# Moving a quarter of the softmax normalisation, the context copies and two waits in a Flamingo-style kernel

## The chip, the cores and the metric

The kernel runs on one core of a Trainium2 chip. The metric is the device time of one execution in microseconds, lower is better. Durations and starts come from one profiled execution; starts count from the first instruction. TensorE (PE), VectorE (DVE), ScalarE (ACT), GpSimd (POOL) and SyncE (SP) each work through a queue of their own in order, and wait for each other on semaphores.

## The reference, cut to what matters

Four layers, each an attention and a feed-forward part, on x of 32 x 128 x 128, with a context of 32 x 77 x 128, all in float32. The change touches the attention of layer 0 and of layer 3:

```python
# layer 0: 16 heads of 8, queries from the normalised x, keys and values from the context
Q, K, V = heads(LN(x) @ Wq + bq), heads(ctx @ Wk + bk), heads(ctx @ Wv + bv)
attn = softmax(Q @ K.T / sqrt(8))                      # over the 77 context rows
x = x + tanh(g_xattn[0]) * (merge(attn @ V) @ Wo + bo)
# then 8 experts, top 2 of each token, on LN(x)
# layer 3: 8 heads of 128, keys and values from the 77 context rows and the 128 rows of x
kv_in = concat([LN(ctx), LN(x)], axis=1)               # 205 rows
attn = softmax((LN(LN(x)) @ Wq + bq) @ (kv_in @ Wk + bk).T * 128 ** -0.5)
x = x + tanh(g_xattn[3]) * (merge(attn @ (kv_in @ Wv + bv)) @ Wo + bo)
```

## The kernel before, in words

The program is a row of phases with a barrier between them. `head_attention` is layer 0's attention, `sparse_experts` its experts, and `latent_attention` layer 3's attention. Each attention phase walks over the 32 batch elements in a software pipeline written out by hand. In `head_attention`, step b does for each engine the front part for batch b+1 (projections), the middle for batch b (scores, exponentials, sums), the back for batch b-1 (transposed probabilities) and the tail for batch b-2 (output projection, residual). Steps 4 to 11 run in a hardware loop, two to an iteration; the others are unrolled, since they also carry the routing of the first 16 batches to the experts.

The order on each engine is that of the code. For a step of `head_attention` it is as follows.

- PE: transpose of `xn` (L667), scores (L675), heads' outputs (L693, the tail's first part), in routing steps four transposes of `xn_ffn` (L700), projections for V, Q, K (L651, L653, L655), the transposes of the 16 heads' probabilities in four groups (L640, `transposes`), the first before and the second after the matmuls that subtract the maximum (L711), the output projection (L730), then the third and fourth group.
- ACT: `xt` (L470), `heads_out` (L477), `v_padded` (L488), `qt` (L494), transposed probabilities of group 0 (L460), in routing steps `xt_ffn` (L504), exponentials (L508), groups 2 and 3 (L460), in routing steps `xn_ffn` (L521).
- DVE: maximum (L548), masked keys (L556), `xn` for batch b+2 (L560), transposed probabilities of group 1 (L565), residual (L570), routing arithmetic, sum (L611), reciprocal (L614).
- POOL: the copy of batch b+2's context into `context_slot` (L426), the output bias on the residual (L430), from step 24 on three scatters of routed rows to `sorted_x` (L437), then the normalisation of batch b in four groups of four heads (L445), which waits for the reciprocal.

Routing lies in steps 14 to 24: `xn_ffn` in steps 15, 16, 17 and 19, its transposes in 16, 17, 18 and 20 (`TRANSPOSE_STEPS`), the choice of experts in 22 (`PICK`), the ranks in 23 (`COUNT`), and 32 scatters from 24 (`SCATTER`) to 33. The phase ends when its last engine ends.

In those steps PE's second group (bank 5) has to wait for ACT's `xt_ffn`, since `xn_ffn`'s transposes lie in the same bank:

```python
if g == 1 and routes and isinstance(b, int) and b in TRANSPOSE_STEPS:
    pe.wait_ge(s["route_xts"], TRANSPOSE_STEPS.index(b) + 1)
```

In `latent_attention` PE transposes the probabilities of a batch in four parts (L2515: context rows of heads 0 to 3 in bank 6, of heads 4 to 7 in bank 4, x's rows of heads 0 to 3 in bank 5, of heads 4 to 7 in bank 6). ACT copies the first and third (L2274, L2276), DVE the second and fourth (L2387, L2389). Then come, for each half of the heads, a product with the context rows (L2524) and one with x's rows (L2525), both into bank 4 + half. Queries for the next batch (L2535), the output projection (L2543) and the scores (L2475) follow. Steps 2 to 11 are in a hardware loop, the others unrolled.

## Time and profile before

| | |
|---|---|
| device time, median of 3 (lowest, highest) | 1610.8 us (1609.99, 1611.7) |
| the profiled execution | 1607.57 us |
| its span, first to last instruction | 1605.8 us |
| busy share of the span: PE, DVE, POOL, ACT | 86%, 63%, 47%, 46% |
| layer 0's attention | about 23 to 255 us |
| layer 3's attention | about 970 to 1384 us |
| mean granted TensorE clock | 0.932 of full speed |

The span is 1.8 us less than the time of that execution, and its time is 3.2 us below the median. An engine's idle time is put down to what released it ("<-"). A start in the rows further down is that of the first instruction of a group; where more are merged, the duration is from the first start to the last end. Neighbouring instructions of an engine overlap somewhat, so the distance from start to start is the rate at which the engine works.

### The profile page before, as it was taken

How to read it: one execution, taken by the hardware profiler on the slowest of the kernel's cores; microseconds unless marked ns; L12 is line 12 of the kernel's file. 1: busy time of each engine (PE TensorE's matmuls, PEld its weight loads, DVE VectorE, ACT ScalarE, POOL GpSimd, SP SyncE). 2: the span in 40 equal slices, each digit the busy share in tenths (PEclk: the TensorE clock that was granted, in tenths of full speed). 3: DMA queues.
4: the chain of work that ended last, by engine and by line, in shares of the span. 5: the costliest groups of instructions: out<-in, count | busy, mean ns of one | idle time of the engine just before them, and what ended most of it. 6: DMA issues, size and time to landing. Idle time of an engine off the chain costs nothing. (4 is left out here: it accounts for less than half of the span.)

```text
span 1605.8 us, 33990 instructions
## 1 busy us (share of the span) xinstructions
PE 1376.9 (86%) x10919; PEld 1113.0 (69%) x10919; DVE 1004.9 (63%) x2272; ACT 732.2 (46%) x1831; POOL 757.8 (47%) x989
## 2 busy tenths in 40 slices
PE   4998776989765796999989978999999999686996
PEld 2776655989755573777746657778887788486984
DVE  4887872413478386999859964455656655353555
ACT  3677453323266544666645532544554544321121
POOL 2554582244273263555534414445444677116445
PEclk9999898999957796999989998999999999798998
DMA  6400033759310000000000000000000000475943
GB/s 185 196 1 1 10 108 89 213 166 273 93 40 13 1 1 1 1 0 0 1 1 1 0 1 1 1 0 0 1 2 1 16 16 17 128 217 171 301 140 85
DMA packets 96491, 100.09 MB, mean 62 GB/s; under 512 B 12149, under 2 KB 69677, under 8 KB 95726
## 3 DMA queue, kind: packets, MB, share of 16 engines
q1 hardware_dynamic: 62322, 69.60, 14.4%
q0 software_dynamic: 8192, 16.79, 3.5%
q10 hardware_dynamic: 25852, 12.09, 2.7%
q8 instruction: 71, 1.16, 0.3%
q14 instruction: 54, 0.44, 0.1%
HBM read 72.23 MB, written 26.21 MB: 61 GB/s over the span
## 5 line engine op out<-in xcount | busy, mean ns | idle before, releaser
L2235 POOL TENSOR_TENSOR exp_scores_xattn<-exp_scores_xattn,softmax_recip_xattn 128x1640 f32<-128x1640 f32 x32 | 93.5, 2921 | 162.8 <-DVE softmax_recip_xattn L2408 162.8
L1470 PE MATMUL psum<-sorted_transposed_ffn,tile_weights_up_ffn 128*128 128x128 f32 x1280 | 164.1, 283 | 5.2 <-DVE sorted_transposed_ffn L1358 5.1
L1470 PEld LDWEIGHTS psum<-sorted_transposed_ffn,tile_weights_up_ffn 128*128 128x128 f32 x1280 | 153.6, 196 | 12.3 <-DVE sorted_transposed_ffn L1358 12.0
L1244 POOL DMA_INDIRECT gathered_rows_ffn<-sorted_y,slot_ffn x96 | 90.7, 944 | 104.6 <-DMA sorted_y<-expert_rows_ffn 46.1
L799 POOL TENSOR_TENSOR exp_scores<-exp_scores,softmax_recip 128x308 f32<-128x308 f32 x128 | 97.5, 783 | 78.9 <-DVE softmax_sum L893 78.9
L1480 PE MATMUL psum<-expert_weights_down_ffn,hidden_ffn 128*128 x960 | 124.4, 281 | 3.3 <-issue 2.9
L1233 POOL DMA_INDIRECT sorted_x<-xn_ffn,slot_ffn x64 | 61.3, 958 | 132.1 <-DVE slot_ffn L1118 113.2
L445 POOL TENSOR_TENSOR exp_scores<-exp_scores,softmax_recip 128x308 f32<-128x308 f32 x128 | 85.7, 701 | 79.2 <-DVE softmax_recip L614 79.1
L1480 PEld LDWEIGHTS psum<-expert_weights_down_ffn,hidden_ffn 128*128 128x128 f32 x960 | 116.7, 196 | 5.2 <-issue 5.2
L2284 ACT ACTIVATE exp_scores_xattn<-psum,scaled_negated_max_xattn 128x205 f32<-128x205 f32 x256 | 106.6, 451 | 0.0
L2475 PE MATMUL psum<-kv_transposed_xattn,queries_xattn 128*128 128x205 f32 x512 | 98.0, 347 | 3.4 <-DVE queries_xattn L2413 3.4
L640 PE MATMUL psum<-identity,exp_scores 128*77 128x128 f32 x512 | 80.2, 283 | 21.1 <-POOL exp_scores L445 13.5
L2262 ACT COPY kv_transposed_xattn<-psum 128x205 f32<-128x205 f32 x32 | 10.6, 332 | 191.5 <-PE psum L2488 191.5
L1273 ACT ACTIVATE hidden_ffn<-psum 128x512 f32<-128x512 f32 x80 | 47.7, 597 | 110.0 <-PE psum L1470 109.8
L2475 PEld LDWEIGHTS psum<-kv_transposed_xattn,queries_xattn 128*128 128x128 f32 x512 | 91.0, 197 | 4.0 <-DVE queries_xattn L2413 3.9
L933 PE MATMUL psum<-identity,exp_scores 128*77 128x128 f32 x512 | 80.4, 281 | 3.1 <-POOL exp_scores L799 1.1
L640 PEld LDWEIGHTS psum<-identity,exp_scores 128*77 128x77 f32 x512 | 60.6, 151 | 31.2 <-issue 21.5
L1279 ACT ACTIVATE silu_ffn<-psum 128x512 f32<-128x512 f32 x40 | 23.9, 597 | 124.5 <-PE psum L1470 124.5
L2355 DVE TENSOR_REDUCE negated_max_xattn<-psum 128x4 f32<-128x820 f32 x64 | 64.7, 1011 | 25.3 <-PE psum L2475 24.9
L1388 DVE COPY expert_rows_ffn<-psum 128x256 f32<-128x256 f32 x80 | 34.0, 425 | 74.0 <-PE psum L1480 67.6
L1358 DVE COPY sorted_transposed_ffn<-psum 128x256 f32<-128x256 f32 x80 | 33.7, 422 | 72.3 <-PE psum L1448 72.2
L2524 PE MATMUL psum<-probs_t_context_xattn,kv_kept_xattn 77*128 77x512 f32 x128 | 68.0, 612 | 9.2 <-ACT probs_t_latents_xattn L2276 8.4
(391 smaller groups left out, 3639.3 us busy)
## 6 DMA issues: line engine op xcount, KB each, us to landing
tile_weights_up_ffn<-in_L_ffn_packed_dram SPq DMA_DIRECT2D x160, 256.0 KB, 3.4
sorted_rows_ffn<-sorted_x SPq DMA_DIRECT2D x80, 128.0 KB, 4.0
sorted_y<-expert_rows_ffn ACTq DMA_DIRECT2D x80, 128.0 KB
sorted_x<-zeros SPq DMA_DIRECT2D x4, 1280.0 KB, 13.3
x_residual<-in_x_dram SPq DMA_DIRECT2D x4, 512.0 KB, 10.9
expert_weights_down_ffn<-in_L_ffn_packed_dram SPq DMA_DIRECT2D x8, 256.0 KB, 14.6
sorted_x<-xn_ffn,slot_ffn POOLq DMA_INDIRECT x128, 2.3
gathered_rows_ffn<-sorted_y,slot_ffn POOLq DMA_INDIRECT x128, 3.0
```

The lines of the kernel that those rows point to most:

```text
L445: nc.gpsimd.tensor_tensor(e[:, par, heads, :], e[:, par, heads, :], rec.to_broadcast([S, HG, KC]), ALU.mult).then_inc(s["probs_ready"], 1)
L640: last = nc.tensor.transpose(m.psum[0:KC, 4 + g % 2, h * S:(h + 1) * S], e[:, nxt, g * HG + h, :], m.ident[:, :])
L799: nc.gpsimd.tensor_tensor(ev, ev, recip[:, ring % 2, :].unsqueeze(1).to_broadcast([S, HG, KC]), ALU.mult).then_inc(s["probs_ready"], 1)
L933: last = nc.tensor.transpose(m.psum[0:KC, 4 + g % 2, h * S:(h + 1) * S], e[:, (ring - 2) % RING, g * HG + h, :], m.ident[:, :])
L1244: nc.gpsimd.indirect_dma_start(yg[:, n % 4, k, :], None, m.sorted_y[half][:, :], bass.IndirectOffsetOnAxis(slot[:, half, k, b:b + 1], 0)). ...
L1470: mm = nc.tensor.matmul(m.psum[:, 2 * (n % 2) + half, to:to + SUB], w[:, n % DEPTH, u, at:at + 128], xst[:, n % 2, u * SUB:(u + 1) * SUB], ...
L1480: mm = nc.tensor.matmul(m.psum[:, 4 + n % 2, u * D:(u + 1) * D], hid[:, n % 2, c, u * 128:(u + 1) * 128], columns(n, u, c * D), start=(c = ...
L2235: nc.gpsimd.tensor_tensor(ev, ev, recip[:, par, :].unsqueeze(2).to_broadcast([S, H3, KV]), ALU.mult).then_inc(s["probs_ready"], 1)
L2284: ins = nc.scalar.activation(e[:, par, h, :], m.psum[:, h // HB, (h % HB) * KV:(h % HB + 1) * KV], ACT.Exp, scale=SCALE, bias=shift_bias[: ...
L2355: nc.vector.tensor_reduce(negmax[:, par, heads].rearrange("p (n h) -> p n h", h=HB), sv, AX.X, ALU.max, negate=True).then_inc(s["negmax_re ...
L2475: mm = nc.tensor.matmul(m.psum[:, h // HB, (h % HB) * KV:(h % HB + 1) * KV], q[:, par, h, :], kvt[:, par, :], start=True, stop=True)
L2524: nc.tensor.matmul(m.psum[:, 4 + half, :], kept[0:KC, nxt, 0, :], ptc[:, cols], start=True, stop=False)
```

## The change

**Layer 0.** The copy into `context_slot` moves from POOL (ahead of the bias) to ACT (behind group 3) in all steps. On POOL, from step 24 on, the three scatters come behind the normalisation instead of ahead of it. Of batches 24 to 31, POOL normalises groups 0 to 2, and ACT normalises group 3, a step later, in four instructions of one head each, between `qt` and group 0's copy; PE's fourth group and DVE's reciprocal of two batches later wait for them. In steps 22 and 23 (`RELIEF`), ACT makes `xn` (behind `xt`) and copies group 1 (behind the exponentials) in DVE's place. In the four `TRANSPOSE_STEPS`, ACT's `xt_ffn` copy comes ahead of group 0's copy instead of behind it.

**Layer 3.** Before, the first matmul of half 0 waited for both of ACT's copies and the first of DVE's; that of half 1 for all four. Now each product waits for its own operand and for its bank to be free.

```diff
@@ head_attention
+    RELIEF = (PICK, COUNT) if routes else ()
+        def shared(b):
+            return routes and isinstance(b, int) and SCATTER <= b < B
@@ POOL, step
-                    if ahead(b, front):
-                        wait(pool, s["v_in_psum"], b + 1)
-                        nc.gpsimd.tensor_copy(cts[:, par, :], m.ctx_t[:, bass.ds((b + 2) * KC, KC)]).then_inc(s["ct_ready"], 1)
...
+                        for g in range(NG - 1 if shared(b) else NG):
...
@@ ACT, step
+                    if ahead(b, front) and at in RELIEF:
+                        wait(act, s["xt_in_psum"], b + 1)
+                        nc.scalar.activation(xn[:, par, :], m.x[:, b + 2, :], ACT.Identity, scale=m.rstd[:, b + 2:b + 3],
+                                             bias=m.shift[:, b + 2:b + 3]).then_inc(s["xn_ready"], 1)
...
-                    if back:
-                        copy_group(b, 0)
                     if at in TRANSPOSE_STEPS:
...
                         nc.scalar.copy(r.xts[:, g % 2 * GT:(g % 2 + 1) * GT], m.psum[:, 5, :]).then_inc(s["route_xts"], 1)
+                    if back and shared(b - 1):
+                        act.wait_ge(s["recip_ready"], b)
+                        for hd in range((NG - 1) * HG, HEADS):
+                            ins = nc.scalar.activation(e[:, nxt, hd, :], e[:, nxt, hd, :], ACT.Copy, scale=recip[:, nxt, hd:hd + 1])
+                        ins.then_inc(s["probs_by_scalar"], 1)
+                    if back:
+                        copy_group(b, 0)
...
                     if back:
+                        if at in RELIEF:
+                            copy_group(b, 1)
                         copy_group(b, 2)
                         copy_group(b, 3)
+                    if ahead(b, front):
+                        wait(act, s["v_in_psum"], b + 1)
+                        nc.scalar.copy(cts[:, par, :], m.ctx_t[:, bass.ds((b + 2) * KC, KC)]).then_inc(s["ct_ready"], 1)
...
@@ DVE, step
-                    if ahead(b, front):
+                    if ahead(b, front) and at not in RELIEF:
...
-                    if back:
+                    if back and at not in RELIEF:
...
+                        if shared(b - 2):
+                            dve.wait_ge(s["probs_by_scalar"], b - 1 - SCATTER)
@@ PE, transposes
+                    if g == NG - 1 and shared(b - 1):
+                        pe.wait_ge(s["probs_by_scalar"], b - SCATTER)
...
@@ latent_attention, PE
                         for half in range(2):
+                            wait(pe, s["pt_read_act"], b * 2 - 1 + half)
+                            wait(pe, s["pt_read_dve"], b * 2 - 1)
+                            cols = slice(half * 512, (half + 1) * 512)
+                            nc.tensor.matmul(m.psum[:, 4 + half, :], kept[0:KC, nxt, 0, :], ptc[:, cols], start=True, stop=False)
                             wait(pe, s["pt_read_act"], b * 2)
                             wait(pe, s["pt_read_dve"], b * 2 - 1 + half)
-                            cols = slice(half * 512, (half + 1) * 512)
-                            nc.tensor.matmul(m.psum[:, 4 + half, :], kept[0:KC, nxt, 0, :], ptc[:, cols], start=True, stop=False)
                             nc.tensor.matmul(m.psum[:, 4 + half, :], kept[:, nxt, 1, :], ptl[:, cols], start=False, stop=True).then_inc(s["c_in_psum"], 1)
```

What now stands in the engines' queues: first POOL at the end of `head_attention`, before, from step 29 to the last scatter (L430 bias, L437 scatters, L445 normalisation, L426 context copy).

```order
L426 COPY context_slot<-context_transposed 128x77
L430 TENSOR_TENSOR x_residual<-x_residual,L_bo_row 128x128
L437 DMA sorted_x<-xn_ffn,slot_ffn 5120x128 x3
L445 TENSOR_TENSOR exp_scores<-exp_scores,softmax_recip 128x308 x4
L430 TENSOR_TENSOR x_residual<-x_residual,L_bo_row 128x128
L437 DMA sorted_x<-xn_ffn,slot_ffn 5120x128 x3
L445 TENSOR_TENSOR exp_scores<-exp_scores,softmax_recip 128x308 x4
L437 DMA sorted_x<-xn_ffn,slot_ffn 5120x128 x3
L445 TENSOR_TENSOR exp_scores<-exp_scores,softmax_recip 128x308 x4
L437 DMA sorted_x<-xn_ffn,slot_ffn 5120x128 x8
```

The same place of the changed kernel, with its own line numbers (L437 bias, L445 normalisation, L452 scatters).

```order
L437 TENSOR_TENSOR x_residual<-x_residual,L_bo_row 128x128
L445 TENSOR_TENSOR exp_scores<-exp_scores,softmax_recip 128x308 x3
L452 DMA sorted_x<-xn_ffn,slot_ffn 5120x128 x3
L437 TENSOR_TENSOR x_residual<-x_residual,L_bo_row 128x128
L445 TENSOR_TENSOR exp_scores<-exp_scores,softmax_recip 128x308 x3
L452 DMA sorted_x<-xn_ffn,slot_ffn 5120x128 x3
L445 TENSOR_TENSOR exp_scores<-exp_scores,softmax_recip 128x308 x3
L452 DMA sorted_x<-xn_ffn,slot_ffn 5120x128 x11
```

A group and the context copy left POOL's steps, and eleven scatters instead of eight stand behind its last normalisation. Next ACT in one step of the same stretch, before:

```order
L470 COPY xt<-psum 128x128
L477 ACTIVATE heads_out<-psum,L_bias_columns 128x128
L488 COPY v_padded<-psum 77x16x8
L494 ACTIVATE qt<-psum,L_bias_columns 128x128
L460 COPY probs_transposed<-psum 77x512
L508 ACTIVATE exp_scores<-psum 128x1232
L460 COPY probs_transposed<-psum 77x512 x2
```

And ACT in such a step of the changed kernel:

```order
L476 COPY xt<-psum 128x128
L487 ACTIVATE heads_out<-psum,L_bias_columns 128x128
L498 COPY v_padded<-psum 77x16x8
L504 ACTIVATE qt<-psum,L_bias_columns 128x128
L516 ACTIVATE exp_scores<-exp_scores,softmax_recip 128x77 x4
L466 COPY probs_transposed<-psum 77x512
L523 ACTIVATE exp_scores<-psum 128x1232
L466 COPY probs_transposed<-psum 77x512 x2
L532 COPY context_slot<-context_transposed 128x77
```

Four normalising instructions stand between the queries and group 0's copy, and the context copy at the end. The instructions on PE are the same in the same order in both kernels; only its waits differ.

## Rows read from the trace of the kernel before

**Rows 1.** Two stretches: length, busy us of PE, PEld, DVE, ACT, POOL; granted clock.
```profile
192.00:235.00 43.00, 35.85 (x458) 27.28 (x456) 34.56 (x56) 23.78 (x50) 37.26 (x54) 0.98 0.34 102
1000.00:1100.00 100.00, 96.76 (x599) 78.96 (x598) 52.04 (x105) 47.04 (x168) 48.59 (x67) 1.00 0.00 0
```
**Rows 2.** Timeline of POOL, steps 25 and 26: start, duration, instruction, idle before.
```profile
201.13 2.67 POOL L445 TENSOR_TENSOR exp_scores<-exp_scores,softmax_recip 128x308 f32<-128x308 f32 x4
203.75 0.24 POOL L426 COPY context_slot<-context_transposed 128x77 f32<-128x77 f32 x1
...
204.64 1.03 POOL L437 DMA_INDIRECT sorted_x<-xn_ffn,slot_ffn  x1 [0.16 <-issue]
...
208.21 2.68 POOL L445 TENSOR_TENSOR exp_scores<-exp_scores,softmax_recip 128x308 f32<-128x308 f32 x4
```
**Rows 3.** Timeline of POOL, first scatter and first shared step, then the phase's end.
```profile
189.55 1.24 POOL L437 DMA_INDIRECT sorted_x<-xn_ffn,slot_ffn  x1 [0.18 <-issue]
...
194.11 0.69 POOL L445 TENSOR_TENSOR exp_scores<-exp_scores,softmax_recip 128x308 f32<-128x308 f32 x1 [0.79 <-DVE softmax_recip L614]
...
242.45 2.66 POOL L445 TENSOR_TENSOR exp_scores<-exp_scores,softmax_recip 128x308 f32<-128x308 f32 x4
...
254.16 0.95 POOL L437 DMA_INDIRECT sorted_x<-xn_ffn,slot_ffn  x1 [0.30 <-issue]
```
**Rows 4.** Timeline of ACT and, in its last line, PE, in plain steps.
```profile
105.79 0.26 ACT L488 COPY v_padded<-psum 77x128 f32<-77x128 f32 x1 [0.42 <-PE psum L655]
105.95 0.37 ACT L494 ACTIVATE qt<-psum,L_bias_columns 128x128 f32<-128x128 f32 x1
106.21 0.58 ACT L460 COPY probs_transposed<-psum 77x512 f32<-77x512 f32 x1
106.72 1.20 ACT L508 ACTIVATE exp_scores<-psum 128x1232 f32<-128x1232 f32 x1
107.81 0.58 ACT L460 COPY probs_transposed<-psum 77x512 f32<-77x512 f32 x1
108.59 0.58 ACT L460 COPY probs_transposed<-psum 77x512 f32<-77x512 f32 x1 [0.20 <-PE psum L640]
...
111.43 0.37 ACT L494 ACTIVATE qt<-psum,L_bias_columns 128x128 f32<-128x128 f32 x1
...
109.33 0.86 PE L693 MATMUL psum<-probs_transposed,v_padded 77*32 77x128 f32 x24
```
**Rows 5.** Timeline of ACT and, in its last line, PE, in a step with `xt_ffn`.
```profile
121.27 1.65 ACT L521 ACTIVATE xn_ffn<-x_residual,x_second_shift,x_second_rstd 128x128 f32<-128x128 f32 x4
122.82 0.25 ACT L470 COPY xt<-psum 128x128 f32<-128x128 f32 x1
...
125.22 0.60 ACT L504 COPY xt_ffn<-psum 128x512 f32<-128x512 f32 x1
...
125.91 0.53 PE L640 MATMUL psum<-identity,exp_scores 128*77 128x128 f32 x3 [0.69 <-issue]
```
**Rows 6.** Timeline of PE and DVE in step 22, then DVE in step 23.
```profile
167.83 0.39 PE L730 MATMUL psum<-L_wo,heads_out 128*128 128x128 f32 x2
...
168.06 0.68 DVE L565 COPY probs_transposed<-psum 77x512 f32<-77x512 f32 x1
...
180.26 0.69 DVE L565 COPY probs_transposed<-psum 77x512 f32<-77x512 f32 x1 [1.46 <-PE psum L640]
```
**Rows 7.** Waits of PE in layer 3's attention: total us, times, longest.
```profile
PE psum L2524 <- ACT probs_t_latents_xattn L2276: 8.4, 30, 0.4
```
**Rows 8.** Timeline in layer 3: a loop step, an unrolled step, DVE's copy and PE.
```profile
1064.83 0.69 DVE L2387 COPY probs_t_context_xattn<-psum 77x512 f32<-77x512 f32 x1
...
1065.99 0.69 PE L2524 MATMUL psum<-probs_t_context_xattn,kv_kept_xattn 77*128 77x512 f32 x1 [0.41 <-ACT probs_t_latents_xattn L2276]
...
1256.24 0.68 DVE L2387 COPY probs_t_context_xattn<-psum 77x512 f32<-77x512 f32 x1
...
1257.28 0.67 PE L2524 MATMUL psum<-probs_t_context_xattn,kv_kept_xattn 77*128 77x512 f32 x1 [0.21 <-ACT probs_t_latents_xattn L2276]
```

25 lines of the change are left out of this document (14 added, 11 removed).

## The prediction, made before the changed kernel ran

> **What bounds the kernel now.** I read the busy time of stretches first, then the timeline of each engine in one step of the kind that the change touches, then the list of waits. In layer 3's attention PE is busy 96.8 of 100 us at full clock, and no other engine more than 52 [rows 1]: what PE idles there is what can be had. Nearly all waits of its first context product are for ACT's copy of x's rows, 8.4 us in 30 of 32 batches [rows 7]. They come in two sizes, 0.41 us in the ten loop steps and 0.21 in the twenty unrolled ones that waited for ACT [rows 8]. In layer 0's attention there are several regimes. In plain steps ACT starts on `qt` every 5.48 us (105.95 to 111.43) and has gaps [rows 4]; PE sets the pace there. In the `TRANSPOSE_STEPS` PE stands still for 0.69 us before the second group of transposes [rows 5]. From step 24 POOL is the bound: 37.3 us busy in 43 without the gaps between its scatters [rows 1], and one normalisation follows the next after 7.08 us with no wait for the reciprocal [rows 2]. POOL also ends the phase, at 254.16 + 0.95 = 255.11 [rows 3].
>
> **Layer 3: the split waits.** Nothing is added or removed but waits. The first product needs ACT's first copy, DVE's first copy (it reads the bank that the product overwrites) and the end of the transposes. In the unrolled step DVE's copy ends at 1256.24 + 0.68 = 1256.92, while PE fell idle at 1257.28 - 0.21 = 1257.07, so the product can follow the transposes at once: the 0.21 goes. In the loop step DVE's copy ends at 1065.52 and PE fell idle at 1065.58. These are close, and a wait in the loop may take a little longer to be seen; I take back 0.33 of the 0.41, with 0.2 and 0.41 as bounds. ACT's second copy is then wanted only behind two matmuls of the first product, which take over 0.8 us, long after it has landed. Sum: 10 x 0.33 + 20 x 0.21 = 7.5 us. PE's gain is everybody's only where PE is next in line; in the few steps with routing arithmetic DVE or POOL ends last, so I take off 1.0 as an estimate: **-6.5 us**. Bounds: 4.2 (the unrolled steps alone) and 8.4 (all of rows 7). The added waits are for things long done, and are hidden behind the running matmul. If DVE is late, this cover is gone and the wait is only renamed.
>
> **Layer 0: the shared steps.** POOL's step was 4 groups at 0.655 = 2.62 ((203.75 - 201.13)/4 each), context copy and bias 0.89 with their gaps (203.75 to 204.64), and three scatters 3.57 (to 208.21) [rows 2]. Now it is three groups 1.96, a gap of 0.17, scatters 3.57, bias 0.45: 6.15 us instead of 7.08. But what is late next? The chain through ACT: from `qt` to group 0's copy 0.26; from there to group 3's copy without its idle 2.08 (0.51 + 1.09 + 0.48); from that to PE's heads' outputs 0.74 (108.59 to 109.33); and on to the next `qt` 2.10 (109.33 to 111.43). That is 5.18 us [rows 4], to which four normalising ACTIVATEs are added between `qt` and group 0's copy, 4s. No row has this form. Bounds for s: 0.16, the distance from a copy without operands per partition to the next instruction (105.79 to 105.95) [rows 4], and 0.39, that of four ACTIVATEs with two such operands and 128 columns ((122.82 - 121.27)/4) [rows 5]. The nearest row is `qt`, one such operand and 128 columns, 0.26 [rows 4]; I take that. The chain is 6.22, just above POOL's 6.15, so a step takes 6.22.
>
> The Trainium skill (ScalarE: Activation LUTs, "What ACT_TABLE_LOAD costs") gives an ACTIVATE 186 ns + 0.833 per column + 93 per pointer operand, less 93 back to back; for 77 columns and one pointer that is 250 ns, which puts the chain at 6.18 and the sum 0.2 us lower. The trace agrees for two pointers and 128 columns: it shows 0.39 between starts, the page gives 386 ns.
>
> The price of the new order: batch 24's three scatters no longer fill POOL's idle time ahead of 194.11 (from 189.55 [rows 3]) but come behind, so eleven scatters instead of eight are left after the last normalisation. Before, the last part took 255.11 - 242.45 = 12.66. One group less (-0.66), three scatters more at 0.96 + 0.30 = 1.26 (+3.78) and no other change: 15.78. From batch 25's normalisation at 201.13: five steps of 6.22, a last one of 5.70 (no bias, no queries), then 15.78: 201.13 + 31.1 + 5.7 + 15.8 = 253.7, against 255.1: **-1.4 us**. With s = 0.16 POOL's 6.15 binds: -1.8. With s = 0.39 the step is 6.74: +1.2.
>
> A scatter can cost more in its new place. The first one took 1.24 us [rows 3], the one of step 25 1.03 [rows 2]; I count 0 and keep 0.2 a step, some +1.4 in all, as the other end. The Trainium skill (SBUF — State Buffer, "Who interferes with whom") says that VectorE in a two-port mode and GpSimd lock each other out for a whole instruction; by it, `xn` on DVE, now beside the first scatter of a step, would make the higher price the rule. The sum would be -0.0 instead of -1.4.
>
> **Layer 0: smaller edits.** `xt_ffn` ahead of group 0's copy starts one copy (about 0.5 us) earlier. PE's wait of 0.69 falls to 0.2, in four steps: **-2.0 us** (bounds 0 and 4 x 0.69 = 2.8). Group 0's copy comes later by as much, but PE wants it only behind the second group, and the exponentials start where they did. The context copy leaves POOL, where in plain steps it lay in idle time, for ACT. In plain steps it stands behind group 3's copy; the next thing on ACT's chain waits for PE, so it is hidden; it also delays `xt` by 0.16, which PE wants only behind the heads' outputs. In steps 14 to 19, ACT goes from there to table loads and `xn_ffn`, for which PE waits: 6 x 0.16 = **+1.0** (bounds 0 and 1.5). The first copy delays the first `xt` by 0.16: **+0.2**. The relief of DVE: in step 22 its copy ends at 168.74 while the output projection that the residual needs ends at 168.22 [rows 6], so the chain of routing comes some 0.4 earlier: **-0.4**. In step 23 DVE had waited 1.46 us before that copy [rows 6]: PE is late there, nothing is won. ACT has room for both instructions.
>
> **Sum.** Layer 3 -6.5, layer 0 -1.4 - 2.0 + 1.0 + 0.2 - 0.4 = -2.6: -9.1 us. The span of 1605.8 becomes 1596.7, the profiled execution's 1607.57 becomes 1598.5. That execution lies 3.2 below the median of 1610.8; the median becomes **1601.7**.
>
> **The rivals.**
> 1. ACT binds the shared steps, or the scatters grow dearer, or the context copy delays more than counted: with s = 0.39 layer 0 gives 0.0 in all, and 1604.3 comes out. For it: the chain and POOL are within 0.1 us of each other, so any slip shows. Against: one pointer operand and 77 columns should cost less than that row.
> 2. In layer 3 the wait is renamed: DVE's first copy, or what a wait in the loop costs, takes the place of ACT's. Then the loop gives 0 and the unrolled half, 2.1; with layer 0's 2.6 that is 1606.1. Against: in the unrolled step DVE's copy ended 0.15 before PE fell idle [rows 8].
> 3. More than forecast: all of the 8.4, and layer 0 with POOL's pace, 2.8 for the copies and little for the context: -13, 1597.8.
> 4. Slower, by one mechanism: the four normalising ACTIVATEs on ACT's chain. The stretch breaks even where six steps take 41.3 - 3.1 = 38.2 us together, a step of 6.45 us (s = 0.32). To eat also the other gains of 7.7 us and 3.2 us more, the step must be 8.3 us, s = 0.78. At s = 0.8 the time is 1614.5. No ACTIVATE of this width is that slow in the rows.
> 5. The change doesn't do what it says: neither stretch is set by what I name, and the gains fall into slack elsewhere: 1609.
>
> **How the numbers follow.** Chances: forecast 0.48, rival 1 0.20, rival 2 0.13, rival 3 0.10, rival 4 0.05, rival 5 0.04. The range from 1597.0 to 1606.5 takes in rivals 1 to 3 and the bounds of layer 3's term with either end of layer 0's, and leaves out rivals 4 and 5 and the edges of 2 and 3, under 2 in 10. A difference of 0.2% (3.2 us) is about what a measurement can tell from none, so faster means under 1607.6: forecast, rivals 1 and 3 whole but for 0.01, and 0.10 of rival 2: 0.87. The same: the rest of these and rival 5: 0.08. Slower: 0.05.
>
> **What would show it.** In layer 3, PE's waits before its first context product fall from 8.4 us to under 2, a loop step loses 0.3 us, an unrolled one 0.2, and PE waits nowhere anew. In layer 0, normalisations on POOL follow each other after 6.2 us, POOL waits a little for the reciprocal in most of these steps, the four ACTIVATEs are 0.26 apart, and POOL ends about 2.6 us earlier than 255.1. The 0.69 us before the second group falls to 0.2. Wrong would be: a new PE wait for DVE of 0.2 or more in layer 3; ACT's normalisations over 0.39 apart; plain steps of layer 0 longer than 5.5 us, which would put the context copy on their path.

## The result, and the profile of the changed kernel

| | before | after |
|---|---|---|
| median of 6 runs each (lowest, highest) | 1610.35 us (1608.38, 1611.7) | 1598.91 us (1597.44, 1603.12) |
| profiled execution, and its span | 1607.57, 1605.8 us | 1598.82, 1596.8 us |
| mean granted TensorE clock of that execution | 0.932 | 0.931 |

The ratio of the mean times is 0.9937, with a 95% interval from 0.9927 to 0.9948: faster by 10.1 us (8.4 to 11.8); the medians lie 11.4 apart. The forecast was 1601.7 with a range from 1597.0 to 1606.5, so the median lies inside it, 2.8 us under the forecast. The profiled execution of before was a quick one: its 1607.57 us lie below the lowest of the six runs. Measured again, the changed kernel gave a median of 1597.66 us over five runs, without a sixth of 1708.03 us that ran at a lower granted clock (0.81).

Layer 3 first. These are PE's waits for ACT in the changed kernel's layer 3, where [rows 7] had 8.4 us in 30 (total us, times, longest):

```profile
PE psum L2550 <- ACT probs_t_latents_xattn L2302: 1.3, 7, 0.2
```

No wait for DVE has taken its place. The timeline of a loop step around the first context product (start, duration) shows why. It answers the first two lines of [rows 8]:

```profile
1061.26 1.93 PE L2541 MATMUL psum<-identity,exp_scores_xattn 128*77 128x128 f32 x16
...
1062.43 0.69 DVE L2413 COPY probs_t_context_xattn<-psum 77x512 f32<-77x512 f32 x1
1062.77 0.59 ACT L2302 COPY probs_t_latents_xattn<-psum 128x512 f32<-128x512 f32 x1 [0.29 <-PE psum L2541]
1063.22 0.69 DVE L2415 COPY probs_t_latents_xattn<-psum 128x512 f32<-128x512 f32 x1
...
1063.27 1.10 PE L2550 MATMUL psum<-probs_t_context_xattn,kv_kept_xattn 77*128 77x512 f32 x2
...
1064.20 1.02 PE L2553 MATMUL psum<-probs_t_latents_xattn,kv_kept_xattn 128*128 128x512 f32 x2
```

The transposes end at 1063.19 and DVE's copy at 1063.12; the product starts at 1063.27, while ACT's second copy is still running (to 1063.36). That second copy is wanted only at 1064.20. So ACT is off the path, and DVE is just not on it: 0.07 us were left. In the unrolled step PE goes from transposes to product without a gap:

```profile
1249.21 1.98 PE L2541 MATMUL psum<-identity,exp_scores_xattn 128*77 128x128 f32 x16
1251.18 1.10 PE L2550 MATMUL psum<-probs_t_context_xattn,kv_kept_xattn 77*128 77x512 f32 x2
```

From the first start of a batch's context products to that of the next batch it was 12.40 us in the loop before and is 12.10 now (12.15 and 12.05 in turn); in an unrolled step it was 12.24 and is 12.02. From PE's first scores of the phase to the start of its last output projection it was 408.0 us and is 400.6.

Layer 0. First the busy time of the two stretches of [rows 1] (length; busy us of PE, PEld, DVE, ACT, POOL; granted clock):

```profile
192.00:235.00 43.00, 39.69 (x479) 30.03 (x479) 35.16 (x60) 32.99 (x89) 35.49 (x46) 0.99 0.33 103
1000.00:1100.00 100.00, 98.79 (x616) 80.78 (x615) 56.92 (x110) 48.27 (x174) 48.49 (x66) 1.00 0.00 0
```

PE goes from 35.85 to 39.69 and from 96.76 to 98.79, ACT in layer 0 from 23.78 to 32.99. A shared step on POOL, in the place of [rows 2], and the last scatter of the phase, in that of [rows 3]:

```profile
213.20 2.00 POOL L445 TENSOR_TENSOR exp_scores<-exp_scores,softmax_recip 128x308 f32<-128x308 f32 x3
215.36 1.01 POOL L452 DMA_INDIRECT sorted_x<-xn_ffn,slot_ffn  x1 [0.16 <-issue]
216.68 0.96 POOL L452 DMA_INDIRECT sorted_x<-xn_ffn,slot_ffn  x1 [0.30 <-issue]
217.94 0.96 POOL L452 DMA_INDIRECT sorted_x<-xn_ffn,slot_ffn  x1 [0.30 <-issue]
218.92 0.47 POOL L437 TENSOR_TENSOR x_residual<-x_residual,L_bo_row 128x128 f32<-128x128 f32 x1
219.34 2.01 POOL L445 TENSOR_TENSOR exp_scores<-exp_scores,softmax_recip 128x308 f32<-128x308 f32 x3
...
252.20 0.95 POOL L452 DMA_INDIRECT sorted_x<-xn_ffn,slot_ffn  x1 [0.30 <-issue]
```

Normalisations follow each other after 219.34 - 213.20 = 6.14 us instead of 7.08, with no wait for the reciprocal, and POOL ends at 253.15 instead of 255.11. The same step on ACT, with the new row L516:

```profile
213.97 0.37 ACT L504 ACTIVATE qt<-psum,L_bias_columns 128x128 f32<-128x128 f32 x1
214.23 1.10 ACT L516 ACTIVATE exp_scores<-exp_scores,softmax_recip 128x77 f32<-128x77 f32 x4
215.23 0.57 ACT L466 COPY probs_transposed<-psum 77x512 f32<-77x512 f32 x1
...
217.73 0.27 ACT L532 COPY context_slot<-context_transposed 128x77 f32<-128x77 f32 x1
...
220.09 0.37 ACT L504 ACTIVATE qt<-psum,L_bias_columns 128x128 f32<-128x128 f32 x1
```

The four ACTIVATEs take (215.23 - 214.23)/4 = 0.25 us each, and the next `qt` comes 6.12 us after this one. POOL and ACT go at the same pace, within 0.02 us.

What the rows do not show by themselves is how much each part gave: the start of layer 3 moved by only 0.5 us (974.2 to 973.7) although POOL's scatters end 2.0 us earlier. The experiments take the parts apart.

### The profile page after: what moved, and what is told of

It reads as the page before. It is cut to its first block and busy times, and to the rows that moved or that the text cites. A ratio compares the mean times of both kernels' runs of the same rounds, so it can differ in the third digit from the quotient of the medians.

```text
span 1596.8 us, 34083 instructions
## 1 busy us (share of the span) xinstructions
PE 1382.9 (87%) x10919; PEld 1118.7 (70%) x10919; DVE 1009.6 (63%) x2268; ACT 742.6 (47%) x1899; POOL 746.9 (47%) x949
## 3 DMA queue, kind: packets, MB, share of 16 engines
q8 instruction: 71, 1.16, 0.3%
## 5 line engine op out<-in xcount | busy, mean ns | idle before, releaser
L825 POOL TENSOR_TENSOR exp_scores<-exp_scores,softmax_recip 128x308 f32<-128x308 f32 x128 | 97.6, 785 | 79.6 <-DVE softmax_sum L919 79.6
L445 POOL TENSOR_TENSOR exp_scores<-exp_scores,softmax_recip 128x308 f32<-128x308 f32 x120 | 80.5, 702 | 91.0 <-DVE softmax_recip L637 91.0
L855 ACT COPY probs_transposed<-psum 77x512 f32<-77x512 f32 x96 | 56.0, 587 | 42.2 <-PE psum L959 41.6
```

Source lines behind the costliest of these rows:

```text
L445: nc.gpsimd.tensor_tensor(e[:, par, heads, :], e[:, par, heads, :], rec.to_broadcast([S, HG, KC]), ALU.mult).then_inc(s["probs_ready"], 1)
L825: nc.gpsimd.tensor_tensor(ev, ev, recip[:, ring % 2, :].unsqueeze(1).to_broadcast([S, HG, KC]), ALU.mult).then_inc(s["probs_ready"], 1)
```

## The experiments

Layer 0 is read below by the starts of DVE's reciprocal of each batch (L614 before, L637 after). The table has the distances between them in us: "4 to 13" is from that of batch 4 to that of batch 13.

| kernel | 4 to 13 | 13 to 15 | 15 to 20 | 21 to 22 | 23 to 24 | 25 to 31 | 31 to the end of the last scatter |
|---|---|---|---|---|---|---|---|
| before | 51.21 | 12.66 | 36.39 | 8.20 | 8.05 | 40.42 | 14.22 |
| after | 51.87 | 12.82 | 35.24 | 7.80 | 8.58 | 35.98 | 16.71 |
| the changed kernel again | 51.89 | 12.81 | 35.25 | 7.81 | 7.87 | 36.03 | 16.8 |
| filler copy on POOL | 51.01 | 12.81 | 35.24 | 7.81 | 8.79 | 35.93 | 16.7 |
| context copy on POOL | 51.22 | 12.65 | 34.45 | 7.82 | 7.87 | 35.96 | 16.7 |
| first trio early | 51.91 | 12.81 | 35.24 | 7.81 | 7.87 | 35.84 | 12.94 |
| two operands per partition | 51.86 | 12.81 | 35.24 | 7.81 | 8.69 | 38.16 | 16.15 |
| no relief | 52.05 | 12.82 | 35.23 | 8.20 | 8.77 | 35.99 | 16.7 |
| only `xt_ffn` moved | 51.03 | 12.66 | 34.45 | 8.20 | 8.79 | 40.09 | 14.2 |
| scatters ahead | 52.01 | 12.82 | 35.23 | 7.80 | 7.87 | 35.85 | 12.9 |
| four scatters early | 51.01 | 12.65 | 34.46 | 7.80 | 8.78 | 35.83 | 11.67 |

All the kernels with 51.0 to 51.2 in the first column have a copy of 77 columns on POOL ahead of the bias add, all with 51.9 to 52.1 have none. The kernel of the first experiment below, whose layer 0 is that of before, has 51.00; the 51.21 of before holds one step of 6.07 us (batch 5 to 6) that took 5.92 there. That step takes one or the other in kernels of either kind, so 0.15 us in this column tell nothing.

**Layer 3's waits alone.** The kernel before, with:

```
 for half in range(2):
+    wait(pe, s["pt_read_act"], b * 2 - 1 + half)
+    wait(pe, s["pt_read_dve"], b * 2 - 1)
+    cols = slice(half * 512, (half + 1) * 512)
+    nc.tensor.matmul(m.psum[:, 4 + half, :], kept[0:KC, nxt, 0, :], ptc[:, cols], start=True, stop=False)
     wait(pe, s["pt_read_act"], b * 2)
     wait(pe, s["pt_read_dve"], b * 2 - 1 + half)
-    cols = slice(half * 512, (half + 1) * 512)
-    nc.tensor.matmul(m.psum[:, 4 + half, :], kept[0:KC, nxt, 0, :], ptc[:, cols], start=True, stop=False)
     nc.tensor.matmul(m.psum[:, 4 + half, :], kept[:, nxt, 1, :], ptl[:, cols], start=False, stop=True)
```

> The kernel before with one part of the change: layer 3's split waits, nothing in layer 0. Theory: this part is worth what the phase showed in the trace of the changed kernel, 7 to 7.5 us between PE's first scores and its last output projection of layer 3 (it was forecast at 6.5), so the time is 1603 us, and PE's waits ahead of the first context product fall from 8.4 us to under 2. Rival: part of the 11.4 us by which the medians differ comes from a TensorE clock that falls and rises elsewhere; then this kernel gains either much less than 6 us or nearly all of it.

Measured: 1602.09 us against 1609.67 for the kernel before beside it, ratio 0.9954 (0.9940 to 0.9967). Layer 3 takes 400.4 us from first scores to last output projection. PE's wait is the same as in the changed kernel:

```profile
PE psum L2524 <- ACT probs_t_latents_xattn L2276: 1.3, 7, 0.2
```

The theory holds: this part is worth 7.4 us by the ratio (5.3 to 9.7) and 7.6 by the medians.

Its layer 0 is the same code as in the kernel before, so it also shows how two executions of that code differ: from batch 0 to 1 it takes 5.94 us here and 5.05 there, from 2 to 3 5.48 and 6.09, from 23 to 24 8.78 and 8.05, and the last scatter ends at 255.90 here and at 255.11 there.

**Layer 0's edits alone.** The changed kernel with the lines above put back.

> The changed kernel with layer 3's two waits put back as they were, so that only the edits of layer 0 are left. Theory: POOL's last scatter of layer 0 ends at 253.2 us as in the changed kernel, 2.0 us earlier than before, and the time is 1608.3 us, 2 to 2.5 us under the kernel before; with the layer-3 kernel of this call the two gains add up to the whole. Rival: layer 0's gain is lost in the routing and the experts behind it, and the time is 1610, or it is larger than 2.5 because a later stretch runs at a higher granted clock.

Measured: 1606.58 us against 1609.67, ratio 0.9980 (0.9971 to 0.9989), that is 3.1 us (1.8 to 4.7) less. Its reciprocals lie within 0.1 us of the changed kernel's throughout, its last scatter ends at 253.18. Layer 3 takes 407.8 us, and the old wait is there again (8.2 us in 29). The two parts add up: 7.6 + 3.1 = 10.7, and the whole gave 10.1 (8.4 to 11.8). The trace of before and that of the changed kernel had shown only 2.0 us on POOL's end; against the 255.90 of the experiment above it is 2.7.

**The context copy, and what it had been good for.** Two kernels, both on the changed one. The first makes POOL copy the context once more to an unused tile in the steps below 24; a semaphore of its own orders the copies. The second puts the copy that counts back on POOL for these steps, and leaves ACT's from step 24 on:

```
 def step(b, par, front, middle, back, tail):          # POOL, first kernel
+    if ahead(b, front) and not (isinstance(b, int) and b >= SCATTER):
+        wait(pool, s["v_in_psum"], b + 1)
+        wait(pool, s["spare_done"], b + 1)
+        nc.gpsimd.tensor_copy(spare[:, par, :], m.ctx_t[:, bass.ds((b + 2) * KC, KC)]).then_inc(s["spare_done"], 1)
```
```
 def step(b, par, front, middle, back, tail):          # POOL, second kernel
+    if ahead(b, front) and not (isinstance(b, int) and b >= SCATTER):
+        wait(pool, s["v_in_psum"], b + 1)
+        nc.gpsimd.tensor_copy(cts[:, par, :], m.ctx_t[:, bass.ds((b + 2) * KC, KC)]).then_inc(s["ct_ready"], 1)
...
-    if ahead(b, front):                               # ACT
+    if ahead(b, front) and isinstance(b, int) and b >= SCATTER:
         wait(act, s["v_in_psum"], b + 1)
         nc.scalar.copy(cts[:, par, :], m.ctx_t[:, bass.ds((b + 2) * KC, KC)]).then_inc(s["ct_ready"], 1)
```

> The changed kernel with one POOL copy more in each step below 24: the transposed context is copied once more, to a tile that nobody reads, where the kernel before had its context copy. ACT keeps the copy that counts. Theory: in the changed kernel the bias add on POOL follows the normalisations at once and meets DVE's xn (0.62 us there instead of 0.40), which makes DVE's copy of group 1 and then PE late; with the filler the bias add starts 0.45 us after the normalisations as it did before, xn falls back to about 0.40, and the plain steps 0 to 13 take 0.08 to 0.09 us less each, 1.2 us in all. In the steps 14 to 19 nothing comes back, since there it is ACT that is late: time 1597.7. Rival: the plain steps grew because ACT has one instruction more in the loop, with its address taken from a register; then they stay as they are, the reciprocal of batch 13 starts at 110.6 and not at 109.5, and the time is 1598.9.

Measured: 1600.18 us, ratio 0.9939 (0.9924 to 0.9953). From batch 4 to 13 it takes 51.01 us instead of 51.87. The reciprocal of batch 13 comes at 110.14, not at 109.5 as the theory had it. Batch 1 came 0.4 us later in this execution (42.17 against 41.81), and from there to batch 13 it is 0.85 us less, not the 1.1 that this would need. First a plain step of the changed kernel on DVE, POOL and PE, then the same with the filler; the last line of each is PE's fourth group of transposes:

```profile
73.30 0.62 DVE L581 TENSOR_SCALAR xn<-x_residual,x_rstd,x_shift 128x128 f32 x1
73.85 0.67 DVE L586 COPY probs_transposed<-psum 77x512 f32<-77x512 f32 x1
...
73.39 0.46 POOL L437 TENSOR_TENSOR x_residual<-x_residual,L_bo_row 128x128 f32 x1
...
74.65 0.66 PE L666 MATMUL psum<-identity,exp_scores 128*77 128x128 f32 x4 [0.38 <-DVE probs_transposed L586]
```
```profile
73.49 0.40 DVE L586 TENSOR_SCALAR xn<-x_residual,x_rstd,x_shift 128x128 f32 x1
73.84 0.69 DVE L591 COPY probs_transposed<-psum 77x512 f32<-77x512 f32 x1
...
73.56 0.25 POOL L438 COPY spare_slot<-context_transposed 128x77 f32 x1
73.77 0.45 POOL L442 TENSOR_TENSOR x_residual<-x_residual,L_bo_row 128x128 f32 x1
...
74.66 0.66 PE L671 MATMUL psum<-identity,exp_scores 128*77 128x128 f32 x4 [0.20 <-DVE probs_transposed L591]
```

In the changed kernel the bias add starts 0.09 us after `xn` and ends at 73.85; `xn` ends at 73.92. DVE's copy of group 1 comes later by 0.2, and PE idles 0.38 instead of 0.20 before the fourth group. With the filler it is the copy that starts 0.07 after `xn`. It ends at 73.81 and `xn` at 73.89. So `xn` is late here too, but beside an instruction of 0.25 us and not beside one of 0.46, and takes 0.40. Useless work on POOL thus gives the plain steps 0.86 us back, all that they had lost (51.01 against the 51.00 of the kernel with layer 3's edit alone). That ACT has one instruction more in the loop costs nothing there, since it is still there in this kernel. The first theory holds in kind, with 0.9 us instead of 1.2; the rival falls. In the steps 14 to 19 nothing comes back (12.81 and 35.24), as expected. The time does not show the 0.9 us: the median is 1.3 above the changed kernel's, and its runs spread from 1596.69 to 1601.27.

> The changed kernel with the context copy back on POOL in the steps below 24 and on ACT from step 24 on, where POOL is the bound. Theory: the plain steps give back 1.2 us and the steps 14 to 19 another 1.0 (0.16 each), the shared steps stay at 6.13 us; the last scatter of layer 0 ends at 251.0 instead of 253.2 and the time is 1596.7. Rival: the copy on ACT cost the steps 14 to 19 nothing, and only the 1.2 come back: 1597.7. Second rival: what is won in layer 0 is lost again where the granted clock falls in the stretches between the layers: 1598.9.

Measured: 1599.05 us, ratio 0.9938 (0.9924 to 0.9952). The plain steps give back 0.65 us, or 0.80 without the step from batch 5 to 6, which is one of 6.07 us here; the steps 14 to 19 0.17 + 0.79 = 0.96, or 0.16 for each, and the shared steps stay at 36.0. So the copy on ACT does cost what was forecast there. The last scatter ends at 250.16, 3.0 us earlier than in the changed kernel: 1.6 of these come from the copies, 0.7 from the distance of batch 23 to 24 (7.87 against 8.58, which the next experiment shows to be chance), and the rest from batches 0 to 4. The median shows none of it. In this execution layer 1's attention starts at 441.5, and in the changed kernel's at 442.8, so 1.3 are left. But from the experts' first transposes to there the same code took 183.8 us in one execution and 185.1 in another (next), so that loss can't be put down to the edit. Whether 1.6 us reach the end stays open with this kernel alone.

**The changed kernel again,** unedited.

> The changed kernel as it is, measured again beside the three kernels of this call. Every reading of this study says the same: 1599 us. If it comes out over 1.5 us from that, differences of that size between calls mean nothing, and only kernels of one call are to be compared.

Measured: 1597.66 us, ratio 0.9924 (0.9911 to 0.9937), 1.2 us under 1598.91. So medians that were not taken side by side may be compared down to about 1.5 us and no further. The table shows what differs between these two executions of the same code: in no step from batch 1 to 23 more than 0.05 us, and then 0.7 us from batch 23 to 24. PE's rows in that step, of the changed kernel and then of the repeat (the matmuls that subtract the maximum and a group of transposes, the same instructions in both):

```profile
188.84 1.00 PE L737 MATMUL psum<-negated_max,identity_bf 128*128 128x308 bf16 x4 [1.56 <-DVE negated_max L569]
189.64 1.06 PE L666 MATMUL psum<-identity,exp_scores 128*77 128x128 f32 x4
```
```profile
189.94 0.71 PE L737 MATMUL psum<-negated_max,identity_bf 128*128 128x308 bf16 x4 [1.56 <-DVE negated_max L569]
190.49 0.60 PE L666 MATMUL psum<-identity,exp_scores 128*77 128x128 f32 x4
```

The same transposes take 1.06 us in the first and 0.60 in the second. Between 188 and 192 us the granted clock is 0.64 of full speed in the first and 1.00 in the second. PE had idled in both just before (1.56 us). Of the eleven kernels of the table four show 7.87, six 8.58 to 8.79 and one 8.05, with no pattern in their edits, and the unedited kernel shows both. The same holds for the stretch from the experts' first transposes to layer 1's attention: 183.8 us and 185.1.

**Where the scatters stand.** Two kernels on the changed one. One moves every trio one step earlier, so that the first is issued ahead of batch 24's normalisation. The other puts each trio back ahead of the normalisation of its own step, as before the change:

```
+if routes and isinstance(b, int) and b == SCATTER:     # first kernel, ahead of "if middle:"
+    ...
+    scatter(0, PER_STEP)
 if middle:
     ...
-    for pair in range((b - SCATTER) * PER_STEP, ...):
+    scatter((b - SCATTER + 1) * PER_STEP, min(2 * HBATCH, (b - SCATTER + 2) * PER_STEP))
```

> The changed kernel with every trio of scatters one step earlier: the first three stand ahead of batch 24's normalisation, in POOL's idle time, as they did before the change, and eight instead of eleven are left behind the last normalisation. Theory: the shared steps stay at 6.13 us, the last scatter ends 3 x (0.96 + 0.30) = 3.8 us earlier, at 249.4 instead of 253.2, and PE's wait for the first sorted rows shrinks with it; time 1595.2. Rival: the steps ahead of batch 24 are not POOL's, and the scatters come so late that they push batch 24's normalisation back by up to 3.6 us; then nothing is won, 1599. Second rival: POOL ends earlier as said, but the experts behind it run at a lower granted clock, as with the context copy on POOL (3.0 us earlier there, of which 1.3 were left at 441 us), and half is left: 1597.

Measured: 1594.55 us (1592.11 to 1595.85) beside 1597.66 for the changed kernel, ratio to before 0.9902 (0.9889 to 0.9915). From the last reciprocal to the end of the last scatter it takes 12.94 us instead of 16.71, that is 3.8 less, and the shared steps do not get longer. The medians differ by 3.1 and the means by 3.9, so nearly all of it, as far as these runs can tell, reaches the end. POOL in this kernel, around batch 24:

```profile
188.05 1.16 POOL L441 DMA_INDIRECT sorted_x<-xn_ffn,slot_ffn  x1 [0.18 <-issue]
189.52 0.97 POOL L441 DMA_INDIRECT sorted_x<-xn_ffn,slot_ffn  x1 [0.30 <-issue]
190.79 0.96 POOL L441 DMA_INDIRECT sorted_x<-xn_ffn,slot_ffn  x1 [0.30 <-issue]
192.62 2.01 POOL L453 TENSOR_TENSOR exp_scores<-exp_scores,softmax_recip 128x308 f32<-128x308 f32 x3 [0.86 <-DVE softmax_recip L640]
```

The trio fits into the wait for the reciprocal with 0.86 us to spare. Both rivals fall.

> The changed kernel with each trio of scatters ahead of the normalisation of its step, as before the change; the last group is still ACT's. Theory: POOL does the same work in each shared step in either order, and the steps stay at 6.13 us; the first trio lies in POOL's idle time and eight scatters are left at the end instead of eleven, so POOL ends 3.8 us earlier and the time is 1595, as with the trios moved by one step. Then to put the scatters behind cost 3.8 us and bought nothing. Rival: with the scatters ahead, the probabilities of a batch come 3.6 us later in the step, PE waits for them, and the step becomes longer than POOL's 6.13, at 0.5 us a step by all of the 3.8: time 1599.

Measured: 1594.51 us, ratio 0.9914 (0.9898 to 0.9930). POOL in two shared steps:

```profile
206.55 2.01 POOL L452 TENSOR_TENSOR exp_scores<-exp_scores,softmax_recip 128x308 f32<-128x308 f32 x3
208.53 0.45 POOL L437 TENSOR_TENSOR x_residual<-x_residual,L_bo_row 128x128 f32<-128x128 f32 x1
209.14 1.01 POOL L444 DMA_INDIRECT sorted_x<-xn_ffn,slot_ffn  x1 [0.17 <-issue]
210.45 0.96 POOL L444 DMA_INDIRECT sorted_x<-xn_ffn,slot_ffn  x1 [0.30 <-issue]
211.71 0.95 POOL L444 DMA_INDIRECT sorted_x<-xn_ffn,slot_ffn  x1 [0.30 <-issue]
212.68 2.02 POOL L452 TENSOR_TENSOR exp_scores<-exp_scores,softmax_recip 128x308 f32<-128x308 f32 x3
```

The step is 212.68 - 206.55 = 6.13 us, as with the scatters behind, and 12.9 us are left after the last reciprocal. So the new place of the scatters bought nothing in this kernel and cost 3.8 us; the gain of the shared steps comes from the fourth group on ACT (0.66 us of POOL's step by [rows 2]) and the context copy off POOL (0.24). No kernel takes these two apart in the shared steps.

**How close ACT's chain is.** The changed kernel with a second operand per partition, a bias of zero, on ACT's normalisation (the values are the same):

```
-ins = nc.scalar.activation(e[:, nxt, hd, :], e[:, nxt, hd, :], ACT.Copy, scale=recip[:, nxt, hd:hd + 1])
+ins = nc.scalar.activation(e[:, nxt, hd, :], e[:, nxt, hd, :], ACT.Identity, scale=recip[:, nxt, hd:hd + 1], bias=m.zeros[:, 0, 0:1])
```

> The changed kernel with a dearer form of ACT's normalising instruction: Identity with a bias of zero that is read per partition, two operands per partition instead of one, same values. Measured now: starts 0.25 us apart; with two operands 0.34 to 0.39. Theory: ACT's chain of 5.18 + 4s (5.18 from the rows of before) is then 6.54 to 6.74 us, longer than POOL's 6.13, so the steps of batches 25 to 31 take that, POOL waits 0.4 to 0.6 us for the reciprocal in each, and its last scatter ends 2.5 to 4 us later than 253.2: time 1602. This would show that the chain lies just under POOL in the changed kernel and how steep the loss is where it takes over. Rival: the chain has more slack than its rows say, since PE and DVE overlap parts of it; then the steps stay at 6.13 and the time at 1599.

Measured: 1599.60 us beside 1597.66, ratio to before 0.9939 (0.9926 to 0.9952). ACT in one step, and POOL's wait in it:

```profile
214.86 0.37 ACT L504 ACTIVATE qt<-psum,L_bias_columns 128x128 f32<-128x128 f32 x1
215.12 1.47 ACT L516 ACTIVATE exp_scores<-exp_scores,zeros,softmax_recip 128x77 f32<-128x77 f32 x4
216.48 0.57 ACT L466 COPY probs_transposed<-psum 77x512 f32<-77x512 f32 x1
...
221.34 0.37 ACT L504 ACTIVATE qt<-psum,L_bias_columns 128x128 f32<-128x128 f32 x1
```
```profile
219.98 2.01 POOL L445 TENSOR_TENSOR exp_scores<-exp_scores,softmax_recip 128x308 f32<-128x308 f32 x3 [0.29 <-DVE softmax_recip L637]
```

The price is (216.48 - 215.12)/4 = 0.34, the step 221.34 - 214.86 = 6.48, and 6.48 - 4 x 0.34 = 5.12: the chain without the ACTIVATEs. At 0.25 that makes 6.12, just below POOL's 6.13. So the theory holds in kind: the chain starts to bind right where the changed kernel stands, and from there each 0.01 us on all four ACTIVATEs costs 0.04 us a step. That it binds is shown; the slope is worked out from these two kernels and not measured at a third price. The step is 0.06 shorter than 5.18 + 4s gave, the last scatter ends at 254.68, 1.5 later than 253.15, where at least 2.5 had been expected, and the time moved by 1.9 instead of 3. The range of the runs (1598.37 to 1602.03) overlaps that of the changed kernel, so the time alone would not show it.

**The two small edits.** In one kernel the relief is off (`RELIEF = ()`), on the changed kernel. In the other, `xt_ffn`'s copy ahead of group 0's is the only edit, on the kernel before:

```
-if back:
-    copy_group(b, 0)
 if at in TRANSPOSE_STEPS:
     ...
     nc.scalar.copy(r.xts[:, g % 2 * GT:(g % 2 + 1) * GT], m.psum[:, 5, :]).then_inc(s["route_xts"], 1)
+if back:
+    copy_group(b, 0)
```

> The changed kernel without the relief of VectorE: in steps 22 and 23, xn and group 1's copy are DVE's again, as before the change. Theory: in step 22 they lie ahead of the residual and the routing arithmetic and cost 0.4 us there, nothing in step 23: the reciprocal of batch 22 comes 7.8 + 0.4 us after that of batch 21, and the time is 1599.3, which no median can tell from 1598.9. Rival: DVE waits anyway, and the distance stays at 7.8.

Measured: 1599.20 us, ratio 0.9940 (0.9927 to 0.9952). From batch 21 to 22 it takes 8.20 us instead of 7.80. The theory holds: the relief is worth 0.4.

> The kernel before with one edit: the copy to xt_ffn stands ahead of group 0's copy on ACT. Theory: PE's wait of 0.69 us before the second group of transposes falls to 0.2 in four steps, and from the reciprocal of batch 15 to that of batch 20 it takes 34.4 us instead of 36.4 (in the changed kernel 35.2, of which 0.8 were for the context copy): time 1607.7. Rival: the edit wins nothing by itself, and the shorter steps 16 to 19 of the changed kernel have another cause; then 36.4 stays.

Measured: 1606.43 us against 1609.90, ratio 0.9984 (0.9975 to 0.9993), or 2.6 us (1.1 to 4.0). From batch 15 to 20 it takes 34.45 instead of 36.39. PE's second group, where [rows 5] had 0.69, and ACT's copy ahead of it:

```profile
125.76 0.63 PE L640 MATMUL psum<-identity,exp_scores 128*77 128x128 f32 x4 [0.21 <-issue]
...
125.08 0.58 ACT L502 COPY xt_ffn<-psum 128x512 f32<-128x512 f32 x1
125.55 0.59 ACT L460 COPY probs_transposed<-psum 77x512 f32<-77x512 f32 x1
```

The theory holds: -1.94 us in four steps.

**Better than both.** The context copy on POOL below step 24 and the scatters one step earlier, then the same with four scatters in the gap instead of three:

```
+scatter(0, PER_STEP + 1)                    # at SCATTER, ahead of the normalisation
 ...
+scatter((b - SCATTER + 1) * PER_STEP + 1, 2 * HBATCH if b == B + 1 else (b - SCATTER + 2) * PER_STEP + 1)
```

> The changed kernel with the context copy on POOL below step 24 and each trio of scatters one step earlier. Theory: the gains on POOL add, 3.0 and 3.8 us, and the last scatter ends at 246.4 instead of 253.2; by the time that is 1592 if all of it stays. Rival: the experts and the stretches behind them give back what they gave back with the context copy alone, over half, through the granted clock; then the phase of the scatters ends at 246.4 and the time is 1596.

Measured: 1594.87 us, ratio 0.9899 (0.9886 to 0.9912), as with the scatters alone (1594.55). Neither the theory's 1592 nor the rival's 1596 came out. The last scatter ends at 248.2, not at 246.4. The parts are there (51.02, 34.46 and 12.96 us in the columns of the table), but this execution had the longer step from 23 to 24 (8.79), and batch 1 came 1.5 us later than with the scatters alone. The expectation had taken 3.0 us for the context copy, of which 1.6 were the copy's.

> The kernel with the context copy on POOL below step 24 and the first scatters in POOL's idle time, with four of them there instead of three, so that seven are left behind the last normalisation. Theory: the fourth just fits (4 x 1.27 = 5.1 us in a gap of 5.4) and pushes batch 24's normalisation back by 0.5 at most; from the last reciprocal to the end of the last scatter it takes 11.7 us instead of 12.9, and the time is 1593.8. Rival: the granted clock behind it takes it back: 1594.9 as measured with three.

Measured: 1591.52 us (1591.16 to 1592.76, four runs), ratio 0.9887 (0.9872 to 0.9901). That is the best of all, 2.3 us under the forecast of 1593.8, and its interval does not touch the changed kernel's. From the last reciprocal it takes 11.67 us. POOL:

```profile
191.66 0.96 POOL L444 DMA_INDIRECT sorted_x<-xn_ffn,slot_ffn  x1 [0.30 <-issue]
193.12 2.01 POOL L456 TENSOR_TENSOR exp_scores<-exp_scores,softmax_recip 128x308 f32<-128x308 f32 x3 [0.50 <-DVE softmax_recip L643]
```

Even the fourth scatter fits with 0.50 us to spare, so batch 24 is not late at all. Against the same kernel with three scatters the edit is worth 1.3 us by the trace (12.96 against 11.67); the medians lie 3.3 apart, but their intervals overlap, and why they differ by more than 1.3 is not shown.

## Why the prediction was right, point by point

**Layer 3: right in mechanism, sized 0.9 too small.** Forecast -6.5, measured -7.4 (400.6 against 408.0). The prices per step held: 0.30 in a loop step (forecast 0.33), 0.22 in an unrolled one (0.21); 10 x 0.30 + 20 x 0.22 = 7.4. The step that failed is the 1.0 taken off for the steps with routing arithmetic. The longest of these took 13.86 us before and 13.62 after: they gained like the others. PE's wait fell to 1.3 us (forecast under 2).

**The shared steps: right.** From batch 25's normalisation to the end of the last scatter the forecast was 31.1 + 5.7 + 15.8 = 52.6; it is 253.15 - 200.91 = 52.2, against 53.98 before. So the term is -1.7 instead of -1.4. The price s is 0.25 (forecast 0.26), the chain without it 5.12 (5.18). One term of that chain, the last 0.48 of 2.08, stands in no row: from one copy to the next [rows 4] have 108.59 - 107.81 = 0.78, of which 0.20 are idle, so 0.58. With 0.58 the chain would have been 5.28, further from the 5.12 that the dearer ACTIVATE showed. The binding engine changed with these hundredths: I had ACT just above POOL and POOL waiting a little in most steps; in the changed kernel POOL does not wait, and only the kernel with the dearer ACTIVATE shows the wait. The price of the order was right: 15.79 us after the last normalisation (forecast 15.78), and the two kernels that move the scatters showed that this 3.8 us was given away. The prediction had counted it but not asked what it bought.

The Trainium skill (ScalarE: Activation LUTs, "What ACT_TABLE_LOAD costs") gives a rule from which 250 ns follow for this form and 343 ns for two pointer operands, back to back; these are estimates, and the traces agree, with 0.25 and 0.34.

**`xt_ffn`: right.** Forecast -2.0, -1.94 as the only edit. PE's gap fell to 0.21 (forecast 0.2).

**The context copy: right in the steps 14 to 19, wrong in the plain ones.** Forecast +1.0 there, and 0.96 measured. In the plain steps I counted nothing, since I looked at what the copy does on ACT. The step that failed is the one not made: what its going from POOL does. It made the bias add start with `xn`, and six of the twelve `xn` between 50 and 115 us took 0.61 to 0.63 us instead of at most 0.47. That is 0.7 us from batch 4 to 13 against before, 0.9 against the filler and against the kernel with layer 3's edit alone, and 0.9 is the better figure, since the 51.21 of before holds the longer step from 5 to 6. The forecast had this collision for the scatters of the shared steps, and not for the bias add. The +0.2 for the first `xt` can't be seen: the first reciprocal starts anywhere between 35.66 and 36.59.

The Trainium skill (SBUF — State Buffer, "Who interferes with whom") says that VectorE in a two-port mode and GpSimd hold the shared pair of ports for a whole instruction, and that the other blocks. The trace agrees for `xn` beside the bias add: in all six cases it ends 0.07 to 0.08 us after the bias add does. For the shared steps it was weighed too high. There `xn` meets the normalisation and not the scatter: it takes 0.43 to 0.50 us, ends 0.09 us after POOL's third group, and 0.07 us or more ahead of the scatter (215.29 and 215.36). The first scatter of a step takes 1.01 us; only the first two of step 24 took 1.16 and 1.18. In the filler kernel `xn` does run into the scatter, and neither is held up: `xn` takes 0.34 us from 209.27, the scatter 1.01 from 209.50. The only longer pair lies in step 24 of that kernel (`xn` 0.47, the scatter 1.19). So no run shows the 0.2 us in every step that the prediction kept as the other end.

**The relief: right.** -0.4 in step 22.

**The sum.** The span came out at 1596.8 (forecast 1596.7), 9.0 shorter where 9.1 had been forecast. That this fits to 0.1 us is luck. Layer 3 gave 7.4. In layer 0 the columns of the table that the edits reach, 4 to 20, 21 to 22 and from 25 to the end, give +0.66 + 0.16 - 1.15 - 0.40 - 4.44 + 2.49 = -2.7, near the forecast of -2.6, but POOL's end moved by only 1.95, since the trace of before was quick from batch 0 to 1 (5.05 us against 5.94 in the same code) and from 23 to 24. Between the scatters and layer 3 another 1.5 us of the difference went, and behind layer 3 1.1 came back, without an edit there; the cause of these is open. The two parts make 7.4 + 2.7 = 10.1, which is what the runs gave, so the forecast of the gain was 1.0 too small, nearly all of it layer 3's 0.9. The 2.8 us between forecast and median come from the step that carries the trace over to the median: the profiled execution of before lay 3.2 under its median, that of after 0.1 under its own. As for the rivals: the waits were not renamed, nor did ACT's price exceed what was given; the missing 0.9 of layer 3 was rival 3's. The loss in the plain steps stood as the last warning sign of the prediction, but with another cause in mind, a copy on ACT's path. Its mark of 5.5 us was set wrong: it was read from a single step of 5.48, while the plain steps of the kernel before already took 51.21 / 9 = 5.69 us on average.

## What to carry to other kernels

An instruction that leaves an engine moves everything behind it on that engine. Ask of each what now runs beside it on the other engines: here a copy that was taken off an idle GpSimd made every second step or so 0.2 us longer, by way of VectorE, and a useless copy in its place gave that back. Where one engine was the bound of a stretch, the order of its work within a step was free (6.13 us either way), and what decided was the two ends: put what nobody waits for into the idle time ahead of the stretch, not behind it (3.8 us for three scatters, 1.3 for a fourth). A wait for two things in front of two matmuls is to be split by what each needs; here it gave 7.4 of the 8.4 us that the profile put down to the later one, since the earlier one ended ahead of the engine's own work.

## What the runs showed of the hardware

- `xn` on VectorE (128 x 128, SBUF to SBUF) takes 0.34 us by itself. When an instruction of GpSimd starts within 0.09 us after it, `xn` ends 0.07 to 0.09 us after that instruction: it takes 0.61 to 0.63 beside the addition, 0.38 to 0.40 beside the copy. When the addition starts 0.15 us after it, `xn` takes 0.34 (50.36 and 50.51). So when the two are this close, it is VectorE that is held up, although GpSimd starts later by the trace. Beside a scatter that starts 0.16 to 0.28 us after it (filler kernel, batches 25 to 28), `xn` takes 0.34.
- An ACTIVATE over 77 columns takes 0.25 us from start to start with one operand per partition, and 0.34 with two.
- The same kernel takes 7.87 us from batch 23 to 24 in one execution and 8.58 in another, after the same idle time of PE, since the clock was granted differently. Between executions of unedited code this step, the start of the phase (0.8 us at batch 0) and the stretch with the experts (1.3 us) vary by themselves. From batch 1 to 23 the two executions of the changed kernel agree within 0.05 us in every step; two of the kernel before's layer 0 differ by 0.6 from batch 2 to 3 and by 0.15 from 5 to 6, and otherwise by less than 0.1. A gain of under 1 us is to be read from the steps, and against more than one execution, not from the end of the phase or the median.
